# Experts sorted by token count on the chip, and fewer slots for the last four of eight

## The reference

```python
xf = x.reshape(1024, 512)
logits = xf @ Wg + bg                                   # 8 experts
one_hot = one_hot(argmax(logits, axis=-1), 8)           # one expert for each token
h = gelu(einsum('td,edh->eth', xf, W1))                 # W1: 8 x 512 x 2048
y = einsum('eth,ehd->etd', h, W2)                       # W2: 8 x 2048 x 512
out = einsum('etd,te->td', y, one_hot)
```

## Time and profile before

| | |
|---|---|
| median of 3 runs | 802.04 us (801.05 to 802.4) |
| profiled execution, span from first to last instruction | 799.9 us |
| share of the span by busy time | PE 97%, DVE 78%, ACT 59%, POOL 30% |
| mean granted TensorE clock | 0.989 of full |
| experts (from the gate's logits to the end) | 559.65 to 799.9 us |

### The profile page before, as it was taken

How to read it: one execution, slowest core, us unless ns; L and a number is a source line. 1 busy time by engine, 2 the same in 40 slices (tenths; PEclk the granted TensorE clock), 3 DMA queues, 4 the chain that set the end, 5 groups by cost and what they waited for, 6 DMA issues and landing times.

```text
span 799.9 us, 22201 instructions
## 1 busy us (share of the span) xinstructions
PE 774.2 (97%) x8860; PEld 458.9 (57%) x8860; DVE 624.1 (78%) x990; ACT 470.1 (59%) x847; POOL 239.5 (30%) x413
## 2 busy tenths in 40 slices
PE   9999999999999999999999999996999999999995
PEld 3444545555445555455557544655867866876783
DVE  5977888879787887787768568787887879788870
ACT  4546676656765656665648034246668768866960
POOL 0245334433354333344331200004153232232131
PEclk9999999999999999999999999997999999999998
DMA  8324453344323444233433511102999998998500
GB/s 303 147 64 110 115 150 94 81 108 109 81 56 82 107 108 121 60 87 109 123 56 57 211 53 53 53 0 88 333 366 412 410 354 318 362 343 331 216 32 15
DMA packets 94901, 125.56 MB, mean 157 GB/s; under 512 B 76352, under 2 KB 79168, under 8 KB 83956
## 3 DMA queue, kind: packets, MB, share of 16 engines
q1 hardware_dynamic: 92260, 117.65, 46.0%
q0 software_dynamic: 2576, 7.02, 2.4%
HBM read 100.47 MB, written 6.88 MB: 134 GB/s over the span
## 4 chain that ended last, share of the span: by engine, by line
PE 79%; DVE 11%; ACT 3%; DMA 2%; issue 1%; SPq 1%; POOL 1%; POOLq 0%; DVEq 0%; ACTq 0%
PE bank L1472 58%; PE bank L1867 11%; PE bank L1641 4%; DVE arena L933 3%; PE bank L1839 3%; PE bank L1607 2%; ACT arena L695 2%; DVE arena L989 2%; DVE arena L995 1%; DMA arena<-arena 1%; ACT arena L662 1%; DMA arena<-in_wv_t 1%; PE bank L1826 1%; DVE arena L948 1%; DVE arena L965 1%
## 5 line engine op out<-in xcount | busy, mean ns | idle before, releaser
L1472 PE MATMUL bank<-arena 128*128 128x160 f16 (+9 forms) x3880 | 554.4, 303 | 7.9 <-DVE arena L933 3.6
L1472 PEld LDWEIGHTS bank<-arena 128*128 128x128 f16 (+3 forms) x3880 | 316.1, 99 | 234.5 <-issue 11.3
L662 ACT ACTIVATE arena<-arena 128x256 f16<-128x256 f32 (+5 forms) x302 | 254.1, 889 | 27.2 <-PE bank L1839 10.3
L933 DVE SCALAR_TENSOR_TENSOR arena<-arena 128x2048 f16<-128x2048 f32 (+4 forms) x102 | 200.6, 1988 | 32.0 <-ACT arena L662 31.7
L662 ACT ACTIVATE arena<-bank 128x512 f16<-128x512 f32 x175 | 100.0, 584 | 143.7 <-PE bank L1472 110.3
L933 DVE SCALAR_TENSOR_TENSOR arena<-bank,arena 128x512 f16<-128x512 f32 x174 | 116.8, 682 | 43.9 <-ACT arena L662 40.3
L1867 PE MATMUL bank<-arena 128*128 128x512 f16 x384 | 86.6, 380 | 0.0
L695 ACT ACTIVATE arena<-arena 128x257 f32<-128x257 f32 x128 | 63.5, 498 | 23.1 <-DVE arena L997 23.1
L528 POOL TENSOR_TENSOR arena<-arena 32x1024 f16<-32x1024 f32 (+1 forms) x16 | 34.1, 2134 | 141.2 <-PE bank L1641 139.3
L1867 PEld LDWEIGHTS bank<-arena 128*128 128x128 f16 x384 | 36.2, 98 | 41.1
L545 POOL COPY arena<-arena 32x256 f16 (+1 forms) x128 | 50.3, 393 | 24.0 <-DVE arena L933 11.8
(11 more groups left out here) (116 smaller groups left out, 497.1 us busy)
## 6 DMA issues: line engine op xcount, KB each, us to landing
arena<-in_w SPq DMA_DIRECT2D x64, 1024.0 KB, 7.8
arena<-in_ctx_t SPq DMA_DIRECT2D x15, 1024.0 KB, 5.3
arena<-in_awt SPq DMA_DIRECT2D x3, 1024.0 KB, 7.3
l_dram<-arena SPq DMA_DIRECT2D x4, 512.0 KB, 3.8
x_dram<-arena SPq DMA_DIRECT2D x1, 2048.0 KB, 14.5
arena<-in_wk_t SPq DMA_DIRECT2D x4, 256.0 KB, 4.7
arena<-in_ctx_t SPq DMA_DIRECT2D x4, 256.0 KB, 6.5
arena<-in_wv_t SPq DMA_DIRECT2D x1, 1024.0 KB, 8.3
```

What stands on the lines that cost most here:

```text
L662: return a.activation(dst, src, ACT.Copy, scale=scale)
L933: return v.scalar_tensor_tensor(dst, src, scale, h, ALU.mult, ALU.subtract)
L1472: last = m.matmul(out_ap, w, x, start=(n == 0), stop=(n == len(pairs) - 1))
```

## The change

Experts 0 and 1 stay where they are. Experts 2 to 7 are sorted by their counts on the chip and run in positions 2 to 7. RANK_AT gives the rank that runs in each position: the largest of the six in position 2, the second in 3, then ranks 4, 7, 5 and 6 in positions 4 to 7. Position p has CAPS[p] slots: 160, 160, 160, 160, 136, 112, 136, 120. Positions 5 and 7 have no last part at all (PARTS is 1): no `last_slots`, one gather, one scatter, one residual gather, 8 transposes. Every width in the hidden layer (matmul, gelu, high, low, token copy) becomes that of the position. The flag for a further round compares each sorted count with the slots of its position.

```diff
+CAPS = (160, 160, 160, 160, 136, 112, 136, 120)
+RANK_AT = (0, 1, 2, 3, 4, 7, 5, 6)
+PARTS = [2 if cap > P else 1 for cap in CAPS]
...
@@ sync
+                                     (i["by_expert"], by_expert_consts)):
                         sp.dma_start(dst, src).then_inc(s["gate_landed"], 16)
...
+            def expert_pieces(n, at):
+                e = sp.value_load(order[0:1, bass.ds(at, 1)], min_val=0, max_val=E - 1)
                 for k in range(PIECES):
                     sp.wait_ge(s["e_lo"], n * PIECES + (k - 7))
                     load_piece(n, e, k)
+            sp.wait_ge(s["routed"], 1)
             with sp.Fori(2, E) as e:
                 expert_pieces(e, e)
-            sp.wait_ge(s["routed"], 1)
...
@@ scalar, and the same on vector (gpsimd: parts and counts only)
-                with act.Fori(1, E - 1) as e:
-                    expert(r * E + e)
+                if is_first(r):
+                    for e in range(1, E - 1):
+                        expert(e)
...
@@ vector
-            v.tensor_tensor(own_ids, onehot16.unsqueeze(3).broadcast_to((P, NT, E, 2)),
-                            tok_ids.unsqueeze(2).broadcast_to((P, NT, E, 2)), ALU.mult).then_inc(s["own_done"], 1)
...
+            def expert_order():
+                chained(v.scalar_tensor_tensor(order_key, counts, float(E), key_offset, ALU.mult, ALU.add))
+                chained(v.tensor_tensor(pair_table[:, 0], over_pairs(order_key), along_pairs(order_key), ALU.is_gt))
+                chained(v.reduce_sum(expert_rank, pair_table[:, 0], AX_X))
+                chained(v.tensor_tensor(score, onehot16, by_tile(expert_rank), ALU.mult))
+                chained(v.reduce_sum(token_rank, score, AX_X))
+                chained(v.tensor_tensor(at_position, by_tile(rank_at), by_expert(token_rank), ALU.is_equal))
+                v.tensor_tensor(own_ids, at_position.unsqueeze(3).broadcast_to((P, NT, E, 2)),
+                                tok_ids.unsqueeze(2).broadcast_to((P, NT, E, 2)), ALU.mult).then_inc(s["own_done"], 1)
+                chained(v.tensor_tensor(pair_table[:, 0], along_pairs(rank_at), over_pairs(expert_rank), ALU.is_equal))
+                v.tensor_tensor(pair_table[:, 1], pair_table[:, 0], over_pairs(expert_no), ALU.mult)
+                chained(v.tensor_tensor(pair_table[:, 0], pair_table[:, 0], over_pairs(counts), ALU.mult))
+                v.reduce_sum(order_f, pair_table[:, 1], AX_X)
+                chained(v.reduce_sum(sorted_counts, pair_table[:, 0], AX_X))
+                v.tensor_copy(order, order_f)
+                chained(v.tensor_tensor(sorted_counts, sorted_counts, cap_of, ALU.subtract))
+                chained(v.reduce_max(most, sorted_counts, AX_X))
+                v.tensor_scalar(more_rounds, most, 0.0, None, ALU.is_gt).then_inc(s["routed"], 1)
...
@@ vector, expert
-                    if first and k == 2:
+                    if first and k == 3:
                         take_ids(0)
...
@@ vector, round_
-                    v.reduce_max(most, BE[:, 0:E], AX_X).then_inc(s["chain_dve"], 1)
+                    v.tensor_copy(counts, BE[:, 0:E]).then_inc(s["chain_dve"], 1)
                     dve.wait_ge(s["chain_dve"], next(chain))
-                    v.tensor_scalar(more_rounds, most, float(CAP), None, ALU.is_gt).then_inc(s["routed"], 1)
                     piece_lo(0, 4)
                     for c in range(KC):
                         first_gathered(c)
                     slots(own_rank)
+                    expert_order()
                     piece_lo(0, 5)
...
@@ tensor, expert
-                        last = product(H_BANKS[k % 4][:, f * CAP:(f + 1) * CAP],
-                                       [(w[u][:, c, at:at + P], xs[:, z, c, :]) for c in range(KC)
+                        last = product(H_BANKS[k % 4][:, f * CAP:f * CAP + cap],
+                                       [(w[u][:, c, at:at + P], xs[:, z, c, 0:cap]) for c in range(KC)
...
-                    if first and k == 1:
+                    if first and k == 2:
                         slot_ids(0)
...
-                    if c == KC - 1:
+                    if c == KC - 1 and parts == 2:
                         last.then_inc(s["y_main"], 1)
-                    if c % 2:
+                    if c % 2 and parts == 2:
                         last_slots((c - 1, c))
+                    elif c % 2:
+                        last.then_inc(s["y_ps"], 1)
```

More of the change, by code:

```diff
@@ L154, in perceiver_block @@
         most = keep.take([1], F32)
+        order_key = keep.take([E], F32)
+        by_expert_consts = keep.take([4, E], F32)
+        key_offset, rank_at, expert_no, cap_of = (by_expert_consts[:, n] for n in range(4))
+        counts, expert_rank, sorted_counts, order_f = (keep.take([E], F32) for _ in range(4))
+        order = keep.take([E], I32)
+        pair_table = keep.take([2, E, E], F32)
+        token_rank = keep.take([NT], F32)
+        at_position = keep.take([NT, E], F32)
         more_rounds = keep.take([1], I32)
@@ L250, in perceiver_block, with caps_of, parts_of, rows_before @@
         assert q_off + 4 * PIECE <= wo_off
+        def caps_of(n):
+            return CAPS[n] if isinstance(n, int) else CAP
+        def parts_of(n):
+            return PARTS[n] if isinstance(n, int) else 2
+        def rows_before(n):
+            return 16 * sum(PARTS[:n]) if isinstance(n, int) else n * 32 - 16 * LEAN
+        def fat_before(n):
+            return sum(z == 2 for z in PARTS[:n]) if isinstance(n, int) else n - LEAN
         def is_first(n):
@@ L604, in scatter @@
             def scatter(n, e):
-                for part in range(2):
-                    pool.wait_ge(s["y_out" if part else "y_head"], n + 1)
+                for part in range(parts_of(n)):
+                    if part == 0 and parts_of(n) == 2:
+                        pool.wait_ge(s["y_head"], fat_before(n) + 1)
+                    else:
+                        pool.wait_ge(s["y_out"], n + 1)
                     pool.sem_inc(s["pool_waits"], 1)
@@ L613, in scatter, with gather_tokens @@
                                          ).then_inc(s["scattered"], 16)
-            def gather_tokens(e):
-                for part in range(2):
+            def gather_tokens(n, e):
+                for part in range(parts_of(n)):
                     g.indirect_dma_start(out=x_rows[part], out_offset=None, in_=i["l2_dram"],
@@ new lines, in over_pairs, with along_pairs, chained @@
+            def over_pairs(z):
+                return z.unsqueeze(1).broadcast_to((P, E, E))
+            def along_pairs(z):
+                return z.unsqueeze(2).broadcast_to((P, E, E))
+            def chained(op):
+                op.then_inc(s["chain_dve"], 1)
+                dve.wait_ge(s["chain_dve"], next(chain))
+            def expert_order():
[16 more added lines that the diff above has]
+                v.tensor_scalar(more_rounds, most, 0.0, None, ALU.is_gt).then_inc(s["routed"], 1)
@@ L1405, in expert @@
             def expert(n, prev=True, nxt=True, first=False):
+                slots = slice(0, caps_of(n))
                 if prev:
@@ L1447, in round_ @@
                 expert(r * E, prev=False, first=first)
-                with dve.Fori(1, E - 1) as e:
-                    expert(r * E + e)
+                if first:
+                    for e in range(1, E - 1):
+                        expert(e)
+                else:
+                    with dve.Fori(1, E - 1) as e:
+                        expert(r * E + e)
                 expert(r * E + (E - 1), nxt=False)
@@ L1955, in host_constants @@
         "id_offset": np.tile(np.array([0, 2 * T], np.float32), (P, 1)),
+        "by_expert": np.tile(np.array([[E - e + (T * E * (2 - e) * 2 if e < 2 else 0) for e in range(E)],
+                                       RANK_AT, range(E), CAPS], np.float32), (P, 1, 1)),
         "quarter_offset": np.stack([np.arange(P) // CB, np.arange(P) // CB + 2 * T * KC], 1).astype(np.float32),
```

56 lines of the change are left out of this document (36 added, 20 removed).

## The result

| | before | changed |
|---|---|---|
| median | 801.63 us (801.05 to 802.4, 4 runs) | 791.75 us (790.31 to 795.65, 4 runs) |
| ratio | | 0.9881, 95% interval 0.9858 to 0.9905 |
| span of the profiled execution | 799.9 us | 790.7 us (its time: 792.47) |
| mean granted TensorE clock | 0.989 | 0.984 |

The account below looks back on a forecast made before the run. TensorE was taken to bound the kernel. Terms: -16.6 lean positions and tail, +1.0 wait at position 5, +4.3 wait in expert 0, +1.7 clock, sum -9.6 from 802.04, giving 792.4 us; range 786.3 to 797.

Parts of the forecast that it names:

- The gain: TensorE at positions 4 to 7 and the tail: narrower matmuls and fewer last slots save 16.6 us, 15.6 after a wait.
- the wait of 1.0: Position 5: TensorE waits about 1.0 us because VectorE's splits and copy of the next expert's tokens are late.
- The chain: VectorE in expert 0: the 16 sorting operations of expert_order add 3.3 us; take_ids is done at 581.8, 5.2 later.
- The wait: Expert 0: the second gather of expert 1 lands at 594.2, so TensorE waits 4.3 us before the transposes; bounds 2.2 and 6.6.
- the first takes 3.28: GpSimd in expert 0: the first gather of expert 1 takes 3.28 us, as in the profile before.
- The bound of 6.6 us for the wait: Expert 0: TensorE's wait if the second gather meets the first's 9.8 us, amid five pieces issued at once.
- The clock: Behind the wait in expert 0: TensorE's granted clock falls to the half level, costing 1.7 us; bounds 0 and 2.
- The stall without a cause: TensorE at 600.56 us: a 1.23 us stall without a named cause, assumed to stay as it is.
- The rivals: Small wait in expert 0 (0.10), VectorE, loads or gather worse (0.09), narrow matmul not faster (0.03), slots too few (0.02).
- Straight code and the order of the weights: ScalarE and VectorE get straight code for a loop, SyncE reads expert numbers from memory: no cost taken.
- The counts fit: Sorted counts stay within the slots; rival: one over sends all engines through eight more experts, about 1013 us, chance 0.02.
- A floor for narrow matmuls: Rival at the lean positions: narrower matmuls keep 69.7 ns, so the kernel takes 802.2 us; chance 0.03.

Follow-up runs that it names:

- sort_only: Changed kernel with 160 slots in all positions, so sorting and straight code but no lean expert: 813.29 us, ratio 1.0075 to the kernel before.
- four_136: Changed kernel with 136 slots in each of positions 4 to 7, so every expert keeps its last part: 805.38 us, ratio 0.9985 to the kernel before.
- ids_first: Changed kernel with sorting chain cut in two, slot_ids after group 1, take_ids after group 0, remaining operations behind it: 784.94 us, ratio 0.9791 to the kernel before.
- all_three: Changed kernel with chain cut in two, take_ids after group 0, earlier token copy and an unused first gather: 783.81 us, ratio 0.9776 to the kernel before.
- early_copy_and_ids: Changed kernel with chain cut in two, take_ids after group 0 and earlier token copy, no unused gather: 783.89 us, ratio 0.9782 to the kernel before.
- yield_back: Changed kernel with slot_ids after group 1, take_ids after group 2, VectorE waiting behind take_ids for GpSimd's gathers: 784.6 us, ratio 0.979 to the kernel before.
- warm_back: Changed kernel with slot_ids after group 1, take_ids after group 2, and an unused early gather of row 0: 791.25 us, ratio 0.9873 to the kernel before.
- copy_early: Changed kernel with VectorE's copy of the next expert's tokens ahead of pieces 2 and 3, from expert 1 on: 789.78 us, ratio 0.9852 to the kernel before.
- ids_back: Changed kernel with slot_ids back after group 1 and take_ids after group 2 of expert 0, sorting chain unmoved: 796.16 us, ratio 0.9872 to the kernel before.

## Why the prediction was right

- *The gain.* 2.20, 6.74, 2.20, 4.64 and 0.8 were forecast for positions 4 to 7 and the tail, less 1.0 at position 5; measured 2.32, 5.85 (6.85 less the wait of 1.0), 2.25, 4.76 and 0.90. Sum 16.1 against 15.6. The gain by width was shown apart by sort_only and four_136, the rest by four_136 and the changed kernel, and the wait of 1.0 by moving the copy.
- *The chain.* 3.26 us against 3.3, and take_ids at 582.23 against 581.8, of which 0.56 lies upstream. VectorE had caught up by the last low part, as said.
- *The wait.* 4.74 against 4.3; the second gather landed at 595.15 against 594.2, again with 0.56 from upstream. But the step under it, "the first takes 3.28", was right by luck: in the other runs the same gather took 1.2, 5.9, 6.1 or 10.5 us, by what VectorE did, and the prediction had no term for that. The bound of 6.6 us for the wait was too low: 10.62 was seen.
- *The clock.* Its fall was forecast, its size was not: 2.96 us against 1.7. I had taken the 4 us of gapless work at the half level in the earlier trace rows for the measure; here TensorE worked for some 6 us at that level. The upper bound of 2 was too low.
- *The stall without a cause.* "I let the 1.23 stand as it is" failed: it was gone in the changed kernel, and position 1 took 1.40 less. It does not hang on the wait in expert 0. Without that wait it was 0.95 us (ids_first), 0.13 (all_three, early_copy_and_ids) or absent (yield_back); with the wait it was absent (changed kernel, warm_back, copy_early) or about 0.9 (sort_only, four_136, ids_back). What the stall is was not tried. The missed 1.3 us of clock and this 1.4 cancel, by luck; what is left (0.5 more gain against 0.4 more wait and 0.56 upstream) is small, so the spans differ by 9.2 where 9.6 was forecast.
- *The rivals.* None came about in the median. Straight code and the order of the weights cost nothing that sort_only shows within its 1 us, and yield_back, which has both, ends 16.6 us under the kernel before where the lean positions gain 16.1. The counts fit, since no further round ran. A floor for narrow matmuls did not show down to 112 columns.

## What to carry to other kernels

When a table moves to a later place, follow the longest thread that hangs on it. Here that was not the engine that makes it but an indirect gather with 0.9 us in hand, and 5 us of lateness cost 7.7 with the clock. Make what a gather needs first and everything else behind it, and look at what the engines beside it do while it is issued: here a pause of 1.33 us on VectorE was enough.

Where an engine's work per stage becomes shorter, look for the copy that the next stage waits for: putting it ahead of bulk work that is not yet due cost nothing here and gave 1 us back.

If one kernel's runs spread by 7 us and its neighbours' by 1, look for a wait whose length depends on timing.

## What the runs showed of the hardware that I had not expected

VectorE can hold up the issue of an indirect DMA on GpSimd far beyond one of its own operations. The same first gather took 1.2 us where it began while VectorE stood still or did small operations (ids_first, yield_back). It took 3.46, 5.93, 6.06 and 10.47 us where it began during one of many weight splits in a row, each 2.2 us long with two inputs in SBUF. In the last case it ended 1.1 us after the run of splits did.

It is not a matter of the first gather. In position 6 of the changed kernel a scatter was held for 8.70 us, off the chain; here are GpSimd's row and the first row of VectorE behind a pause:

```profile
741.47 8.70 POOL L642 DMA_INDIRECT out<-arena  x1 [12.94 <-DVE arena L1470]
```

```profile
749.82 0.44 DVE L1486 SCALAR_TENSOR_TENSOR arena<-arena 128x272 f16<-128x272 f32 x1 [0.55 <-ACT arena L695]
```

VectorE had run splits and low parts without a gap up to that pause of 0.55 us, and the scatter ended at 750.17, 0.9 us after the pause began. In ids_back the gather ended 1.1 us behind a pause of 0.1 us, at 584.3. In copy_early the same scatter took 11.61 us and ended 1.0 us after VectorE had turned to the copy out of a bank, which has one input (756.02). But a pause is not always needed: in the changed kernel the gather behind the first began during a split as well (587.34) and took 2.04 us only. When GpSimd is let through and when it is passed over is not shown.

The Trainium skill has the rule ("SBUF — State Buffer", section SBUF: two separate sides): of an operation of VectorE with two SBUF inputs and one of GpSimd that reads SBUF, the one that starts first has the shared port pair for its whole instruction, and the other is blocked. The runs agree in one direction, GpSimd behind VectorE; that this can last over several instructions in a row is what they add. The other direction doesn't show: the split that began 0.29 us after the gather in yield_back took its usual 2.29 us. That it is the second SBUF input that matters was not tried: no run changed VectorE's operation itself.
